# Conditioned residual mixing with a LoRA linear layer, fp32: another order of the opening transfers, tile 0's LoRA in split precision, A of the adapters asked for one step earlier

## The reference

```python
x = x + einsum('bct,bcd->bdt', x, L0_weights[cond])          # L0_weights (16, 32, 32)
A, Bm = lora_As[adapter], lora_Bs[adapter]                    # (64, 512, 16), (64, 16, 512)
x = x + einsum('bti,oi->bto', x, W) + bias \
      + 2 * einsum('btr,bro->bto', einsum('bti,bir->btr', x, A), Bm)
```

## Time and profile before

| | |
|---|---|
| profiled execution, device time | 84.99 us |
| its span, first to last instruction | 83.2 us |
| around the span | 1.79 us |
| busy: TensorE, weight loads, VectorE, ScalarE, POOL | 79.4, 72.2, 60.2, 52.3, 33.7 us |
| mean granted TensorE clock | 1.000 |
| DMA traffic | 16.07 MB, 193 GB/s mean |
| remainder of b on VectorE (L470), of half an A (L465) | 692, 284 ns |
| rounding of b on ScalarE (L378), of half an A (L372) | 632, 300 ns |

### The profile page before, as it was taken

How to read it: one execution, slowest core, us unless ns; L and a number is a source line. 1 busy time by engine, 2 the same in 40 slices (tenths; PEclk the granted TensorE clock), 3 DMA queues, 4 the chain that set the end, 5 groups by cost and what they waited for, 6 DMA issues and landing times.

```text
span 83.2 us, 2011 instructions
## 1 busy us (share of the span) xinstructions
PE 79.4 (95%) x524; PEld 72.2 (87%) x524; DVE 60.2 (72%) x158; ACT 52.3 (63%) x179; POOL 33.7 (41%) x75
## 2 busy tenths in 40 slices
PE   4999999999999999999999999999999999999970
PEld 2378897899899999999999999999999999999850
DVE  2059765977789687777878787978777777869560
ACT  1553947954867675957666766667585867665620
POOL 6118842871171717080625344351708071304300
PEclk9999999999999999999999999999999999999999
DMA  1899786796987888765768766576764526030334
GB/s 15 287 357 311 203 233 200 211 278 195 335 254 182 262 199 227 194 212 201 176 195 213 219 195 234 156 264 183 230 188 150 174 85 189 17 119 0 126 126 126
DMA packets 16141, 16.07 MB, mean 193 GB/s; under 512 B 10241, under 2 KB 10626, under 8 KB 16130
## 3 DMA queue, kind: packets, MB, share of 16 engines
q1 hardware_dynamic: 14016, 11.67, 47.3%
q0 software_dynamic: 1248, 4.06, 15.7%
q10 hardware_dynamic: 866, 0.21, 1.1%
HBM read 11.74 MB, written 4.19 MB: 191 GB/s over the span
## 4 chain that ended last, share of the span: by engine, by line
PE 82%; SPq 6%; DMA 4%; DVE 2%; issue 2%; ACT 0%; DVEq 0%
PE z_ps L570 49%; PE z_ps L607 9%; PE z_ps L650 5%; PE ht_ps L561 5%; DMA a_raw<-in_lora_a 4%; PE y_ps L622 4%; PE y_ps L618 4%; PE y_ps L620 4%; SPq L237 3%; PE ht_ps L594 2%; PE ht_ps L659 1%; DVE y_sb L555 1%; SPq L227 1%; SPq L234 1%; SPq L257 1%
## 5 line engine op out<-in xcount | busy, mean ns | idle before, releaser
L570 PE MATMUL z_ps<-wa,x_hi 128*128 128x288 f32 (+2 forms) x240 | 50.2, 301 | 0.0
L570 PEld LDWEIGHTS z_ps<-wa,x_hi 128*128 128x128 f32 x240 | 37.9, 188 | 2.0 <-issue 0.5
L570 PE MATMUL z_ps<-wa,x_lo 128*128 128x288 f32 (+2 forms) x120 | 35.2, 295 | 0.0
L570 PEld LDWEIGHTS z_ps<-wa,x_lo 128*128 128x128 f32 x120 | 22.5, 188 | 0.0
L309 POOL CAST m_hi<-m_raw 128x128 fp32r<-128x128 f32 x16 | 4.9, 303 | 35.4 <-ACT m_raw L346 35.4
L300 POOL DMA_INDIRECT b_raw<-in_lora_b,b_index_slot x16 | 16.8, 1048 | 4.4 <-POOL b_index_slot L298 4.4
L490 DVE TENSOR_TENSOR z_lo<-z_ps,z_hi 128x256 fp32r<-128x256 f32 x31 | 11.8, 420 | 6.3 <-ACT z_hi L390 6.3
L390 ACT CAST z_hi<-z_ps 128x256 fp32r<-128x256 f32 x31 | 10.2, 376 | 9.5 <-PE z_ps L607 9.5
L346 ACT COPY m_raw<-w_raw 32x32 f32 x64 | 13.8, 216 | 2.1 <-DVE w_raw L522 1.1
L449 DVE TENSOR_TENSOR x_lo<-x_raw,x_hi 128x512 fp32r<-128x512 f32 x14 | 9.7, 691 | 3.5 <-ACT x_hi L358 3.5
L470 DVE TENSOR_TENSOR b_lo<-b_raw,b_hi 128x512 fp32r<-128x512 f32 x15 | 10.4, 692 | 0.6
(11 more groups left out here) (57 smaller groups left out, 78.3 us busy)
## 6 DMA issues: line engine op xcount, KB each, us to landing
out<-y_sb SPq DMA_DIRECT2D x15, 256.0 KB, 2.5
x_raw<-in_xt SPq DMA_DIRECT2D x14, 256.0 KB, 3.0
a_raw<-in_lora_a SPq DMA_DIRECT2D x60, 32.0 KB, 2.6
first_sb<-in_first SPq DMA_DIRECT2D x2, 384.0 KB, 3.7
first_sb<-in_first SPq DMA_DIRECT2D x3, 256.0 KB, 5.2
b_raw<-in_lora_b,b_index_slot POOLq DMA_INDIRECT x16, 3.7
bias_sb<-in_bias SPq DMA_DIRECT2D x1, 256.0 KB, 3.0
a_raw<-in_lora_a ACTq DMA_DIRECT2D x4, 32.0 KB
```

Source lines behind the costliest of these rows:

```text
L570: done = nc.tensor.matmul(target, (x_hi, x_lo)[part[0]][u % 2][:, k, :], moving(part[1]), start=k == 0 and part == HH, stop=k == KC - 1 an ...
```

## The change

Tile 0's LoRA now goes the way of the others: ht0 is masked, rounded (`round_ht0`) and its rest taken (`rest_ht0`), the two parts stand one above the other in the 128 partitions of ht_sb[0], and b of tile 0 is gathered for 128 rows (each twice) and split. The `first` transfers are cut at other places (192, 320, 512, 256 and 256 KB instead of 384, 384, 256, 256 and 256 KB), and the chunks of t are in reverse order everywhere, so that chunk k has its diagonal block in column block 3 - k. The warm-up is 7 products of 512 columns instead of 8 and one of 256. w0 moves from SP's queue to ScalarE's, its identity addition moves ahead in VectorE's order. A of tile 3 is asked for ahead of the loop, A of tile u + 3 in step u, with x of tile u + 3 behind it. The index of tile 0's gather is made in its own instruction. Tile 1's LH products of chunks 0 to 2 stand behind tile 0's h. On the host the layouts are reversed to match (left out below).

```diff
-    WARM_UP = (512,) * 8 + (256,)
+    WARM_UP = (512,) * 7
-    X0_AT = (0, 2 * P + O)
-    W_AT = (2 * P, 4 * P + O, 4 * P + 2 * O, 4 * P + 3 * O)
+    X0_AT = (0, P + O, 2 * (P + O), 3 * P + 2 * O)
+    W_AT = (P, 2 * P + O, 4 * P + 2 * O, 4 * P + 3 * O)
-    PIECES = (0, X0_AT[1], W_AT[2], W_AT[3], X1_AT, X1_AT + T)
+    PIECES = (0, W_AT[0] + HALF, W_AT[1] + HALF, W_AT[3], X1_AT, X1_AT + T)
-    DIAGONAL_HALF = tuple(k * P // HALF for k in range(KC))
+    DIAGONAL = tuple(KC - 1 - k for k in range(KC))
+    DIAGONAL_HALF = tuple(d * P // HALF for d in DIAGONAL)
+    PIECE_OF_DIAGONAL = (1, 2, 2, 3)
...
@@ SP
             load_x(2)
-            sp.dma_start(w0_raw[:, :, :], w0).then_inc(w0_loaded, 16)
             load_a(2)
             load_x(3)
+            load_a(3)
+            sp.dma_start(bias_sb[:, :], bias).then_inc(bias_loaded, 16)
             for u in range(1, TILES):
-                if u + 2 < TILES:
-                    load_a(u + 2)
-                if u == 1:
-                    sp.dma_start(bias_sb[:, :], bias).then_inc(bias_loaded, 16)
-                    load_x(4)
-                if u + 4 < TILES:
-                    load_x(u + 4)
+                if u + NA < TILES:
+                    load_a(u + NA)
+                if u + 3 < TILES:
+                    load_x(u + 3)
                 if u >= 2:
                     store_y(u - 2)
...
@@ POOL, gather_b(u)
-            pool.wait_ge(b_index_ready, 1)
-                if u == NB:
-                    pool.wait_ge(lora_done, 2)
-                elif u > NB:
-                    pool.wait_ge(b_ready, u - NB)
-                rows = slice(0, JR if u == 0 else P)
-                pool.tensor_copy(b_index_slot[s][:, :], b_index[:, u:u + 1]).then_inc(b_index_copied, 1)
-                pool.wait_ge(b_index_copied, u + 1)
+                    pool.wait_ge(b_ready, u - NB + 1)
+                pool.wait_ge(b_index_ready, 1 if u == 0 else 2)
+                if u > 0:
+                    pool.tensor_copy(b_index_slot[s][:, :], b_index[:, u:u + 1]).then_inc(b_index_copied, 1)
+                    pool.wait_ge(b_index_copied, u)
...
@@ ScalarE
             act.dma_start(ids_p_sb[:, :], ids_of_p).then_inc(ids_p_loaded, 16)
+            act.dma_start(w0_raw[:, :, :], w0).then_inc(w0_loaded, 16)
...
+            def round_ht0():
+                act.wait_ge(ht0_masked, 1)
+                act.copy(ht_sb[0][0:JR, :], ht0_sb[:, :]).then_inc(ht0_hi_ready, 1)
...
             round_x(2)
-            round_a(2)
+            round_b(0)
+            round_ht0()
             act.wait_ge(m_zero, 2)
             act.wait_ge(w0_plus_i, 1)
             build_m(0)
+            round_a(2)
...
@@ VectorE
             def add_identity(k):
-                dve.wait_ge(first_loaded[k], 16)
-                diagonal = w_raw(k)[:, k * P:(k + 1) * P]
+                dve.wait_ge(first_loaded[PIECE_OF_DIAGONAL[k]], 16)
+                diagonal = w_raw(k)[:, DIAGONAL[k] * P:(DIAGONAL[k] + 1) * P]
...
+            def rest_ht0():
+                dve.wait_ge(ht0_hi_ready, 1)
+                nc.vector.tensor_tensor(ht_sb[0][JR:P, :], ht0_sb[:, :], ht_sb[0][0:JR, :],
+                                        ALU.subtract).then_inc(ht_ready, 1)
...
-                nc.vector.tensor_scalar(b_index[:, :], ids_p_sb[:, 0:TILES], float(R), r_of_p[:, 0:1],
+                nc.vector.tensor_scalar(b_index_slot[0][:, :], ids_p_sb[:, 0:1], float(R), r_of_p[:, 0:1],
+                                        ALU.mult, ALU.add).then_inc(b_index_ready, 1)
+                nc.vector.tensor_scalar(b_index[:, 1:], ids_p_sb[:, 1:TILES], float(R), r_of_p[:, 0:1],
                                         ALU.mult, ALU.add).then_inc(b_index_ready, 1)
...
                 rest_w(k)
+            (wait for w0, w0 plus identity: moved here)
             rest_x1(0)
             rest_x1(1)
             rest_w(3)
             rest_a(1)
             mask_ht(0)
-            (wait for w0, w0 plus identity)
+            rest_b(0)
+            rest_ht0()
             rest_x(2)
             rest_a(2)
...
@@ TensorE
             def lora(u, half):
-                if u == 0:
-                    pe.wait_ge(b_gathered[0], 16)
-                    nc.tensor.matmul(z_of(0, half), ht0_sb[:, :], b_raw[0][0:JR, cols(half)], start=False,
-                                     stop=True, skip_group_check=True).then_inc(lora_done, 1)
-                    return
-                pe.wait_ge(b_ready, u)
+                pe.wait_ge(b_ready, u + 1)
...
+            def first_chunk(k, half):
+                if half == DIAGONAL_HALF[k]:
+                    pe.wait_ge(w_plus_i, k + 1)
+                else:
+                    pe.wait_ge(first_loaded[k], 16)
...
+            for k, half in ((0, 0), (1, 0), (0, 1), (1, 1), (2, 1), (2, 0), (3, 1), (3, 0)):
+                first_chunk(k, half)
...
             for k in range(2):
                 pe.wait_ge(w_ready, k + 1)
                 half_chunk(1, k, 0, (HH, HL))
-            pe.wait_ge(x_ready, 1)
-            for k in range(2):
-                half_chunk(1, k, 0, (LH,))
             pe.wait_ge(x_hi_ready, 2)
             pe.wait_ge(w_ready, 3)
             half_chunk(1, 2, 0, (HH, HL))
+            first_h()
             pe.wait_ge(x_ready, 2)
-            half_chunk(1, 2, 0, (LH,))
-            first_h()
+            for k in range(3):
+                half_chunk(1, k, 0, (LH,))
```

More of the change, by code:

```diff
@@ L145, in lora_residual_program @@
         ht_computed = sem("ht_computed")
+        ht0_masked = sem("ht0_masked")
+        ht0_hi_ready = sem("ht0_hi_ready")
         ht_ready = sem("ht_ready")
@@ L170, in x0_chunk @@
         def x0_chunk(k):
-            at = X0_AT[k // 2] + k % 2 * P
-            return first_sb[:, at:at + P]
+            return first_sb[:, X0_AT[k]:X0_AT[k] + P]
         def a0_chunk(k):
@@ L375, in round_b @@
                 act.wait_ge(b_gathered[u % NB], 16 * (u // NB + 1))
-                if u >= 3:
+                if u >= 2:
                     act.wait_ge(lora_done, 2 * (u - 1))
@@ L514, in _ @@
                 rest_w(k)
+            dve.wait_ge(w0_loaded, 16)
+            nc.vector.tensor_tensor(w0_raw[:, :, :], w0_raw[:, :, :],
+                                    ident[0:C, 0:C].rearrange("p (a d) -> p a d", a=1).broadcast_to([C, S0, C]),
+                                    ALU.add).then_inc(w0_plus_i, 1)
             rest_x1(0)
@@ L520, in _ @@
             mask_ht(0)
-            dve.wait_ge(w0_loaded, 16)
-            nc.vector.tensor_tensor(w0_raw[:, :, :], w0_raw[:, :, :],
-                                    ident[0:C, 0:C].rearrange("p (a d) -> p a d", a=1).broadcast_to([C, S0, C]),
-                                    ALU.add).then_inc(w0_plus_i, 1)
+            rest_b(0)
+            rest_ht0()
             rest_x(2)
@@ L641, in mix_last_quarter @@
                                  stop=True, skip_group_check=True).then_inc(y_computed, 1)
-            def first_chunk(k):
-                pe.wait_ge(first_loaded[k], 16)
-                for half in (1 - DIAGONAL_HALF[k], DIAGONAL_HALF[k]):
-                    if half == DIAGONAL_HALF[k]:
-                        pe.wait_ge(w_plus_i, k + 1)
-                    nc.tensor.matmul(z_of(0, half), x0_chunk(k), w_raw(k)[:, cols(half)], start=k == 0,
-                                     stop=k == KC - 1, skip_group_check=True)
-            for k in range(KC):
-                first_chunk(k)
+            def first_chunk(k, half):
[3 more added lines that the diff above has]
+                    pe.wait_ge(first_loaded[k], 16)
+                nc.tensor.matmul(z_of(0, half), x0_chunk(k), w_raw(k)[:, cols(half)], start=k == 0,
+                                 stop=k == KC - 1, skip_group_check=True)
+            for k, half in ((0, 0), (1, 0), (0, 1), (1, 1), (2, 1), (2, 0), (3, 1), (3, 0)):
+                first_chunk(k, half)
             def first_h():
@@ L746 @@
     R = lora_a.shape[2]
-    xt = x.reshape(TILES, P, KC, P).transpose(0, 3, 2, 1)
+    xt = x.reshape(TILES, P, KC, P)[:, :, ::-1].transpose(0, 3, 2, 1)
     x0 = xt[0].reshape(P, T)
-    wt = _np.asarray(inputs["L1_cond_W"]).T.reshape(KC, P, -1).transpose(1, 0, 2)
+    wt = _np.asarray(inputs["L1_cond_W"]).T.reshape(KC, P, -1)[::-1].transpose(1, 0, 2)
     ids_of_p = _np.repeat(adapter.reshape(TILES, J).T, C, axis=0)
@@ L754 @@
     laid = {
-        "first": _np.concatenate([x0[:, 0:2 * P], wt[:, 0], x0[:, 2 * P:], wt[:, 1], wt[:, 2], wt[:, 3],
+        "first": _np.concatenate([x0[:, 0:P], wt[:, 0], x0[:, P:2 * P], wt[:, 1], x0[:, 2 * P:], wt[:, 2], wt[:, 3],
                                   xt[1].reshape(P, T)], axis=1),
```

12 lines of the change are left out of this document (6 added, 6 removed).

## The result

The changed kernel takes 86.30 us (median of 5 runs, 85.68 to 88.76) against 84.96 us for the kernel before (84.67 to 85.13): ratio 1.0162, 95% interval 1.011 to 1.0214. It is slower by 1.3 us; forecast was 84.7. A repeat in another job gave 85.93, 86.63, 89.48 and 89.56. Over both jobs the nine runs form two groups: five from 85.68 to 86.63, four from 88.69 to 89.56; the ratio takes the first group alone. Each experiment is compared with the kernel before in its own job, whose median was 84.61 (e1 to e4), 84.63 (e5 to e8), 84.85 (e9 to e12) and 84.65 us (e13 to e15).

What follows compares the result with a forecast made beforehand. TensorE bounds it (busy 79.4 of 83.2 us), apart from standstills. Opening -0.10 and stall -0.33 give -0.43; tile 4's x gives -0.28, and the later limit counts: 84.99 - 0.28 = 84.71, said 84.7, range 84.35 to 85.5.

Steps and rivals of the forecast that it cites:

- The third transfer at 6.08: First transfers: the new third piece lands at 6.08 like the old one, moving add_identity(1) from 5.32 to 6.11.
- the opening at -0.10: Up to step 2: its first weight load at 14.7 instead of 14.80; bounds -0.3 and +0.35, set by the gather.
- Rival D: Opening: TensorE's clock rises later, ten pieces end at 10.8, 1.5 later, about 86.0 us; chance 0.04.
- pieces at 0.425 after 6.5: Tile 0's fp32 pieces on TensorE: still at the slower spacing after 6.5 would show the forecast wrong.
- Around the span 1.79: Device time outside the profile's span: 1.79 us, kept unchanged in the sum of 84.99.
- x4, the term that set the forecast: Tile 4's x, now issued last at 16.70, lands at 19.70 by the 3.0 median: -0.28 us.
- limit L - 19.98: Tile 2's LoRA: time changes by L - 19.98, L being the landing of tile 4's x; bounds 19.4 and 20.5.
- Rival A: Tile 4's x is the new stall: landing at 20.5 costs +0.52, 85.5 us; chance 0.15.
- The stall of 0.33 at tile 4's A: Stall at 22.02, costing about 0.33 us once; A issued 1.1 earlier removes it.
- VectorE's chain: VectorE's in-order opening work: chunk 1's diagonal pushes it 0.8, tile 0's LoRA near 13.2, step 2's first load 14.7.
- The gather: Tile 0's gather of B, 128 rows, issued at 6.8: lands at 11.4, bounds 11.0 and 12.0.
- LoRA in fp32r, four products for 0.48: Tile 0's LoRA: four fp32r products of 256 replace four fp32 pieces (1.25); TensorE's work falls by 0.77.

Runs made afterwards that it cites:

- e1: The changed kernel again, no edit, for a second profile: 85.93, 89.56, 89.48 and 86.63 us.
- e4: The kernel before with only SP's new order (A asked for earlier, bias, tile 4's x behind tile 4's A): 85.08 us, ratio 1.0059.
- e5: The kernel before, unchanged, for a second profile: 84.80 us, ratio 1.0011.
- e8: The changed kernel with the 512 KB third transfer cut in two and w0 in SP's queue behind the first transfers: 85.68 us, ratio 1.0112.
- e9: The kernel before with two more semaphores that nothing uses: 84.59 us, ratio 0.9982.
- e12: e11 with its two added semaphores replaced by later counts of two existing ones: 84.70 us, ratio 0.9966.
- e13: The kernel before with tile 0's gather of B bringing 128 rows in place of 64: 84.71 us, ratio 1.0006.
- e15: The same kernel as e10, measured again: 84.47 us against 84.65 before, ratio 0.9991.
- e2: The changed kernel with w0 issued by SP behind the five first transfers, not in ScalarE's queue: 86.08 us, ratio 1.014.
- e7: The kernel before with only the new cut (transfer sizes, reversed chunks, warm-up, tile 0's product order): median 85.57 us of eleven; ratio 1.0076 for the first seven.
- e3: The changed kernel with the 512 KB third transfer cut in two of 256 KB: 85.59 us, ratio 1.0109.
- e14: The kernel before with tile 0's gather indices made by their own instruction, without POOL's copy, gather at 64 rows: 84.65 us, ratio 1.0003.
- e6: The changed kernel with transfers, warm-up, chunk order and TensorE's order of tile 0 as before: 85.20 us, ratio 1.0072.
- e10: The kernel before with A asked for three tiles ahead, but tile 4's x ahead of bias and tile 4's A: 84.64 us, ratio 0.9971.
- e11: e6 with tile 4's x ahead of bias and tile 4's A: 84.84 us, ratio 1.0014.

## Why the prediction was wrong

1. **The third transfer at 6.08: failed, and with it the opening.** The prediction put the opening at -0.10 with bounds of -0.3 and +0.35; in e1 step 2 begins 1.0 later than before (15.80, 14.80). I took the landing of the same byte count from one row as if it were a constant, and read it 0.09 too high (issued at 1.74, landed at 5.99). With the old cut the profiles show 6.0 to 7.0, with the new 512 KB one 6.77, 7.84, 8.29 and 8.52. In the 88.76 execution fifteen of the sixteen DMA engines have marked the 512 KB as complete by 6.53 and the last one at 8.52. Its packets of 4 KB (those left run one behind the other): one begun at 5.75 takes 944 ns where most take 159, seven more follow until 8.09. In e2 fifteen are there by 6.05 and the last at 8.29, in e7 by 6.78 and at 7.84; in e1 none stands apart (6.75, 6.77). Why one engine falls behind stays open. The Trainium skill, "DMA: Bandwidth & Descriptors", section "Latency and other measured facts", says that engines 7 and 15 are usually slower than the others and has a best guess for it, tied to the descriptor rings of POOL's DMAs. One slow engine is what the traces show too, but they don't name it, and the guess does not cover this case: the transfer is SP's, and POOL issued its first gather at 9.43, after the landing. The old cut has the same hazard with less behind it: e4's third transfer landed at 6.99 (fifteen engines by 6.03) and TensorE paused 0.33. The change put the diagonal of chunk 1, and so VectorE's whole chain, behind this landing; the prediction saw this, priced it at 0.8, and gave the landing no range. w0 in ScalarE's queue, which it put at nothing for this transfer, may be a part of it (6.71 with, 5.60 without: e3, e8), but with it moved neither kernel was clearly faster (e2, e8).
2. **Rival D had nearly the right price and the wrong trigger.** I gave 0.04 to a clock that rises later after a shorter warm-up, on the ground that three times of before lay within 0.28 us. The rise is far from steady: near 6.2 in before, near 7 in e5, 3.9 in e3. The Trainium skill, "TensorE: Matmul & The Clock Gate", Part 1, was cited there for a release that varies between runs; the traces agree. So "pieces at 0.425 after 6.5" was no sign of anything: e5, the kernel before, has them too. What costs is another event: the clock falls again, to 1.2 GHz from 9.34 to 12.75 after the pause of 2.46 us, and from 9.23 to 12.64 in e2 after one of 2.29; the four runs of the changed kernel above 88 all have a mean clock of 0.98 or less. Between the two profiled executions of the changed kernel the landing makes 1.75 us (8.54 - 6.79, the starts of add_identity(1)) and the clock 1.30 (4.11 - 2.81; D had 1.5), together the 3.05 by which tile 0's h is later (13.65, 10.60); 2.86 of it is left at step 5 (32.99, 30.13). That the pause brings the fall rests on two executions with and the others without; whether the shorter warm-up has a part in it was not tested, since every kernel with a pause of over 1 us has it.
3. **"Around the span 1.79": failed by 0.31.** A constant of the program before, not of the chip. It goes with tile 0's LoRA in fp32r (eight profiles with it, nine without) and with what always came with it, the new order of ScalarE's, VectorE's and TensorE's instructions around it. Semaphores (e9, e12), w0's queue (e2, e8), the A order (e4), the cut (e7), the gather's rows (e13) and the index (e14) are excluded one by one. What in the rest does it stays open.
4. **x4, the term that set the forecast: the mechanism right, the size off.** Issue forecast at 16.70, 16.74 in e4; limit L - 19.98. I took a landing of 3.0; ScalarE could start on x4 3.14 after its issue in e4 (19.88) and 3.53 after it in e6 (19.89). With L = 19.88 the formula gives -0.10, not -0.28, and in e6 it cost more than the opening had gained (step 3 to step 4 took 5.16). In the changed kernel itself this limit hardly came into play, since its opening was later: e1 has no wait for x4 (landed 20.52, wanted 20.67), the 88.76 execution one of 0.16. Rival A, that x4 is the new stall, got 0.15; it is what happens in e6, and not in the changed kernel. By the medians the order costs more than the formula has: e4 is 0.5 over before of its job, e10, which differs by the place of x4 and of the x's after it alone, 0.2 under of its own; other executions of e4 probably got x4 later still, which no profile shows.
5. **The stall of 0.33 at tile 4's A: real in that execution, not in the kernel.** Three other profiles with the old order have none, and two have a larger one at tile 5 (0.94 in e14, 0.49 in e7). A stall of one profile is neither a sure gain nor a bound of it.
6. **VectorE's chain: right** in order and in nearly every duration, shifted by step 1's error alone, up to the LoRA at 13.88. The gather too: forecast at 11.4, it landed at 12.13 and held ScalarE to 12.16. Behind the LoRA 0.42 more was lost (15.80 for 14.7, less the 0.68), to something that the prediction does not have, POOL's work of that moment. VectorE before (x remainder, two A remainders), then POOL in e1, to be held against e1's VectorE rows of 13.85 and 14.60 above:

```profile
12.22 0.67 DVE L449 TENSOR_TENSOR x_lo<-x_raw,x_hi 128x512 fp32r<-128x512 f32 x1
12.82 0.47 DVE L465 TENSOR_TENSOR wa<-a_raw,wa 128x128 fp32r<-128x128 f32 x2
```

```profile
13.84 0.29 POOL L311 CAST m_hi<-m_raw 128x128 fp32r<-128x128 f32 x1 [0.53 <-ACT m_raw L349]
14.22 0.78 POOL L313 TENSOR_TENSOR m_lo<-m_raw,m_hi 128x128 fp32r<-128x128 f32 x1
```

VectorE's two groups take 0.83 and 0.75 for 0.67 and 0.47, and POOL's m_lo 0.78 for 0.47 in the profile of before, where it stood beside z's remainders (14.28). It is not that both work at once, which they do in before as well, but on what. Over the seventeen profiles m_lo takes 0.45 to 0.47 us in 265 of 272 places, nearly all of them beside VectorE's z remainder or sum of y, which read PSUM. In the seven where it stands beside A's remainders, with both inputs in SBUF, it takes 0.53 to 0.78, the two longest (e1, e8) with x's remainder beside it too; and x's remainder takes 0.83 in these two and 0.67 to 0.70 in all others.

7. **LoRA in fp32r, four products for 0.48: right for TensorE's work** (16.49 to 16.96 in the 88.76 execution, 13.88 to 14.46 in e1). It is worth little: from the last fp32 piece to step 2's first mixing product the old cut takes 6.71 to 6.91 us with it (e6, e11, e12) and 6.98 to 7.22 without, 0.1 to 0.3 for the 0.77 of work, and the 0.31 outside the span takes that back.

What 86.3 is made of, from e1's 85.93: +0.65 at step 5 (30.13 - 29.48; that is +0.99 at step 2, 16.70 - 15.71, less the 0.33 of the stall) and +0.3 outside the span. The cut alone costs 0.64 by e7. The remaining 0.4 to the median is in no profile; a landing later than 6.79 with a pause that leaves the clock alone, as in e7 (7.84, 86.95), would do it, but that is argued and not shown.

The best versions are e10/e15 (84.64, 84.47) and e12 (84.70), 0.1 to 0.3% under before of their jobs, with intervals that reach 1.0001 or beyond: none is shown to beat the kernel before.

## What to carry to other kernels

A landing time from one profile is a sample: before an in-order engine's whole chain is put behind one transfer, ask what happens if it lands 2 us later, and let the first user of a large early transfer be something that nothing else queues behind. Idle time of TensorE in the opening is priced twice, once as the pause and once as the clock that it may cost. Before two openings are compared, look at when the clock rose in each: here that alone moved the kernel before by 0.4 us between two profiles. A stall seen in one execution should be seen in a second one before its removal is booked as a gain, and a moved load has to be followed on both sides: what it lets go earlier, and what now stands behind it.

## What the runs showed of the hardware that was not expected

- The same program on the same data landed one early transfer of 512 KB at 6.77 in one execution and 8.52 in another, where fifteen of sixteen DMA engines were through by 6.53; a 256 KB one in its place landed at 6.71 and (with w0 moved) 5.60.
- After pauses of TensorE of 2.29 and 2.46 us the granted clock went to 0.50 and was back at 1.00 by 13; after 1.69, 1.39 and 0.34 it stayed at 1.00.
- With TensorE busy from 1.07 on, its pieces went from 0.43 to 0.22 us apart at a moment between 3.9 and 7, near 6.2 and near 7 in two profiles of the kernel before (before, e5), whose openings differ by 0.4 us for it.
- VectorE and POOL working at once, all inputs in SBUF: a pair of 128 x 128 remainders in 0.75 for 0.47, POOL's in 0.78 for 0.47; with VectorE reading PSUM neither is slower.
- The device time outside the profile's span is a property of the program: 1.7 to 1.8 in nine profiles, about 2.1 in the other eight, though every kernel starts its first transfer at 0.82.
